# Low parts of the first two batches shared 3 to 5 between VectorE and GpSimd, and the first batch's keys and queries placed from SBUF to SBUF

## What is computed

```python
def reference(x, ctx1, ctx2, Wq, bq, Wk, bk, Wv, bv, Wp, bp, w_router, w_gating, w_gate, w_up, w_down):
    # x, ctx1, ctx2: (16, 256, 256)
    q = layernorm(x) @ Wq + bq
    k = concat([ctx1 @ Wk + bk, ctx2])            # 512 keys a batch
    v = concat([ctx1 @ Wv + bv, ctx2])
    attn = softmax(q k^T * 16 ** -0.5)            # per batch and head: 256 x 512
    x = x + (attn @ v) @ Wp + bp
    h = layernorm(x)
    cw = softmax(h @ w_router) * softmax(h @ w_gating / 0.1)
    cw = cw / (sum(cw) + 1e-9)                    # 8 weights a token
    for e in range(8):                            # w_gate, w_up: 256 x 1024, w_down: 1024 x 256
        x += cw[:, e] * ((silu(h @ w_gate[e]) * (h @ w_up[e])) @ w_down[e])
    return x
```

## Time and profile before

| | us |
|---|---|
| median of 3 runs | 2712.37 |
| lowest and highest | 2711.29, 2715.34 |
| the profiled execution, its own time | 2711.55 |
| its span in the trace | 2709.8 |
| mean granted TensorE clock | 0.991 of full |

### The profile page before, as it was taken

One profiled execution on the slowest core, in us unless ns is written; L12 is line 12 of the kernel. 1 busy time (PEld: TensorE's weight loads), 2 busy tenths in 40 slices (PEclk: granted clock), 3 DMA queues, 4 the chain that ended last, 5 costly groups with the idle time before them and its releaser, 6 DMA issues.

```text
span 2709.8 us, 46807 instructions
## 1 busy us (share of the span) xinstructions
PE 2660.4 (98%) x15969; PEld 2184.3 (81%) x15969; DVE 2007.7 (74%) x3303; ACT 1526.0 (56%) x2887; POOL 1651.8 (61%) x1837
## 2 busy tenths in 40 slices
PE   6899999999999999999999999999999999999998
PEld 5578888888888888888888888888888888888887
DVE  6987777777778777777777777777787777655554
ACT  4655555555555555555555555555555555544443
POOL 4766666666656666566666566666566666655554
PEclk8899999999999999999999999999999999999999
DMA  6344434444333443433434433444333442333332
GB/s 166 101 112 122 127 100 118 132 120 123 115 118 115 120 126 115 127 109 112 131 115 131 120 116 108 125 122 131 113 105 114 126 122 88 97 107 113 108 102 82
DMA packets 298427, 315.44 MB, mean 116 GB/s; under 512 B 22096, under 2 KB 269264, under 8 KB 298192
## 3 DMA queue, kind: packets, MB, share of 16 engines
q1 hardware_dynamic: 298192, 312.45, 39.0%
HBM read 278.15 MB, written 33.69 MB: 115 GB/s over the span
## 4 chain that ended last, share of the span: by engine, by line
PE 94%; DVE 4%; issue 1%; DMA 1%; POOL 0%; ACT 0%; SPq 0%; POOLq 0%; DVEq 0%; ACTq 0%
PE ps_s L706 26%; PE ps_t L706 26%; PE ps_o L740 25%; PE ps_s L803 4%; PE ps_t L813 4%; PE ps_a L782 2%; PE ps_a L784 2%; PE ps_m L586 1%; PE ps_m L615 1%; DVE negmax L1187 1%; PE ps_m L604 1%; DVE Pt_lo L1059 1%; PE ps_m L659 0%; DMA d_k<-kT_lo 0%; PE ps_m L677 0%
## 5 line engine op out<-in xcount | busy, mean ns | idle before, releaser
L969 DVE SCALAR_TENSOR_TENSOR hf<-hf,ps_s 128x512 f32<-128x512 f32 x512 | 350.2, 684 | 326.7 <-ACT hf L827 324.8
L833 ACT ACTIVATE h_hi<-ps_t 128x512 fp32r<-128x512 f32 x512 | 306.1, 598 | 440.2 <-DVE ps_t L976 440.2
L1221 POOL TENSOR_TENSOR wg_lo<-stage_w,wg_hi 128x512 fp32r<-128x512 f32 x256 | 330.9, 1292 | 339.5 <-ACT wg_hi L840 337.9
L827 ACT ACTIVATE hf<-ps_s 128x512 f32<-128x512 f32 x512 | 306.4, 598 | 410.5 <-PE ps_s L706 410.5
L981 DVE TENSOR_TENSOR h_lo<-ps_t,h_hi 128x512 fp32r<-128x512 f32 x512 | 353.0, 689 | 211.9 <-ACT h_hi L833 205.6
L740 PE MATMUL ps_o<-h_lo,wd_hi 128*128 128x512 f32 x1024 | 400.1, 391 | 0.0
L740 PE MATMUL ps_o<-h_hi,wd_hi 128*128 128x512 f32 x1024 | 398.5, 389 | 0.9 <-DVE h_lo L981 0.9
L740 PE MATMUL ps_o<-h_hi,wd_lo 128*128 128x512 f32 x1024 | 398.4, 389 | 0.0
L976 DVE TENSOR_TENSOR ps_t<-hf,ps_t 128x512 f32<-128x512 f32 x512 | 356.4, 696 | 52.9 <-PE ps_t L706 6.2
L1221 POOL TENSOR_TENSOR wd_lo<-stage_w,wd_hi 128x512 fp32r<-128x512 f32 x256 | 330.8, 1292 | 93.0 <-ACT wd_hi L840 93.0
L947 ACT ACTIVATE Pt<-ps_t 128x512 f32<-128x512 f32 x512 | 305.8, 598 | 142.1 <-PE ps_t L813 134.1
(11 more groups left out here) (208 smaller groups left out, 4734.3 us busy)
## 6 DMA issues: line engine op xcount, KB each, us to landing
stage_w<-in_L_ffn_w_gate_dram SPq DMA_DIRECT2D x256, 256.0 KB, 2.8
stage_w<-in_L_ffn_w_up_dram SPq DMA_DIRECT2D x256, 256.0 KB, 3.1
stage_w<-in_L_ffn_w_down_dram SPq DMA_DIRECT2D x256, 256.0 KB, 2.8
KTs<-d_k SPq DMA_DIRECT2D x96, 256.0 KB, 4.9
cwb<-d_cw SPq DMA_DIRECT2D x64, 256.0 KB, 3.6
QTs<-d_q SPq DMA_DIRECT2D x192, 64.0 KB, 2.7
X<-in_x_dram SPq DMA_DIRECT2D x32, 256.0 KB, 4.5
d_k<-kT_hi SPq DMA_DIRECT2D x16, 512.0 KB, 4.1
```

Source lines behind the costliest of these rows:

```text
L827: act.activation(hf[:], ps_g[:], ACT.Tanh, scale=0.5).then_inc(tanh_done, 1)
L833: act.activation(h_hi[f % FC][:], ps_u[:], ACT.Copy).then_inc(hh_done, 1)
L969: dve.scalar_tensor_tensor(out=hf[:], in0=hf[:], scalar=1.0, in1=ps_g[:], op0=ALU.add, op1=ALU.mult).then_inc(gate_done, 1)
L1221: pool.tensor_tensor(lo[:], raw_weights(n), hi[:].bitcast(F32), ALU.subtract).then_inc(wl_done, 1)
```

## The change

**The low parts.** For items of batches 0 and 1 DVE now takes items 1, 4, 6 of each eight, POOL 0, 2, 3, 5, 7. That is 4 low parts fewer on DVE and 4 more on POOL in each of the two batches, 8 in all. From batch 2 on the shares stay. The semaphores behind the low parts are counted with a running sum.

**The first batch's placing.** For batch 0 the way through DRAM is gone: `place_first` issues, pair by pair, 3 DMAs of keys (32 rows of 2 KB each) and 6 of queries (16 rows of 1 KB each) directly from `kT` and `qT` to `KTs` and `QTs`. These are 72 DMAs on SP, where the old way had 4 stores and 18 loads. PE waits for each pair's own semaphore (`first_in`). ACT and DVE may overwrite `kT` and `qT` for batch 1 only when all 72 have landed (`wait_stored`).

**Around it.** The 3 loads of the experts' weights move from `first_loads` to steps 20 to 22 of turn 0. Of the constant rows only 3 are loaded, and the transposed scores use 99 rows of `KTs` and `QTs` where they used 128. GpSimd's clearing of `key_rows` (0.53 us in the trace) is gone. The q of batch 0 goes to a bank of its own, `ps_t[1]`, and waits for no other projection.

```diff
--- before.py
+++ after.py
     DVE_LOW = (1, 3, 5, 7)
+    DVE_LOW_ALONE = (1, 4, 6)
...
+        first_in = [sem(f"first_in{p}") for p in range(PAIRS)]
...
+        def wait_stored(eng, turn, count):
+
+            if turn.b == 0:
+                for arrived in first_in:
+                    eng.wait_ge(arrived, 16 * 9)
+            else:
+                turn.wait(eng, count, -1, 32)
...
+                if (b, name) == (-1, "q"):
+                    items[b, step] = (name, k, d, None, [])
+                    continue
...
-            return ps_m[:] if one else ps_o[:, 1, :]
+            return ps_t[1][:] if one is None else ps_m[:] if one else ps_o[:, 1, :]
...
-        def by_dve(i):
-            return i % OCT in DVE_LOW
...
+        def by_dve(b, i):
+            alone = (b + 1) * STEPS <= START
+            return i % OCT in (DVE_LOW_ALONE if alone else DVE_LOW)
...
-                for n in range(3):
-                    load_weights(n, 0)
-                eng.wait_ge(const_ready, CONSTS)
-                eng.dma_start(KTs[TOP:P].bitcast(F32), key_rows[TOP:P].unsqueeze(1).broadcast_to([ROWS, PAIRS, NK])).then_inc(rows_in, 16)
+                eng.wait_ge(rows_set, 1)
+                eng.dma_start(KTs[TOP:USED].bitcast(F32), key_rows[TOP:USED].unsqueeze(1).broadcast_to([3, PAIRS, NK])).then_inc(rows_in, 16)
...
+            def place_first():
+
+                eng.wait_ge(k_l.sem, 2)
+                eng.wait_ge(m_l.sem, 1)
+                for pair in range(PAIRS):
+                    m, at = pair // GP, pair % GP * ROWS
+                    for slot, part in enumerate((kT_hi, kT_lo, kT_hi)):
+                        eng.dma_start(KTs[slot * ROWS:(slot + 1) * ROWS, pair, :].bitcast(F32),
+                                      part[at:at + ROWS, m, :].bitcast(F32)).then_inc(first_in[pair], 16)
+                    if pair == 0:
+                        eng.wait_ge(q_l.sem, 2)
+                        eng.wait_ge(const_ready, CONSTS)
+                    for slot, part in enumerate((qT_hi, qT_hi, qT_lo)):
+                        for h in range(2):
+                            to, row = slot * ROWS + h * HD, at + h * HD
+                            eng.dma_start(QTs[to:to + HD, pair, h, :].bitcast(F32),
+                                          part[row:row + HD, m, :].bitcast(F32)).then_inc(first_in[pair], 16)
...
+                    if turn.b == -1 and step == 10:
+                        place_first()
+                    if turn.b == 0 and step >= 20 and step - 20 < 3:
+                        load_weights(step - 20, 0)
...
+                        if turn.b + d == 0:
+                            if i % 4 == 0:
+                                pe.wait_ge(first_in[i // 4], 16 * 9)
...
-                        pe.matmul(key_bank(j)[:], KTs[:, pair, kc * P:(kc + 1) * P],
-                                  QTs[:, pair].rearrange("p h n -> p (h n)"),
+                        pe.matmul(key_bank(j)[:], KTs[0:USED, pair, kc * P:(kc + 1) * P],
+                                  QTs[0:USED, pair].rearrange("p h n -> p (h n)"),
...
-                        turn.wait(act, used, 0, 32)
+                        wait_stored(act, turn, used)
...
-                        turn.wait(dve, used, 0, 32)
+                        wait_stored(dve, turn, used)
```

More of the change, by code:

```diff
@@ L389, in tokens @@
             return xh[g % 2][:, :, k, :], xl[g % 2][:, :, k, :]
-        def by_dve(i):
-            return i % OCT in DVE_LOW
-        def low_parts(i, dve):
-            return sum(by_dve(j) == dve for j in range(i))
+        def by_dve(b, i):
+            alone = (b + 1) * STEPS <= START
+            return i % OCT in (DVE_LOW_ALONE if alone else DVE_LOW)
+        low_parts = {True: [0], False: [0]}
+        for b in range(B):
+            for i in range(STEPS):
+                for dve in (True, False):
+                    low_parts[dve].append(low_parts[dve][-1] + (by_dve(b, i) == dve))
         def raw_weights(n):
@@ L455, in place_queries @@
             def place_queries(turn, d, g):
[L457 removed]
+                turn.wait(eng, q_out, d - 1, 32)
                 turn.wait(eng, t_ps, d - 1, 2 * OCT * (g + 1))
[L459 to L460 removed]
                 pairs = slice(g * GP, (g + 1) * GP)
@@ L500, in body @@
                         combine_ahead(f)
[L501 to L509, removed]
-                    if turn.has(0) and step == 1:
-                        place_keys(turn, 0, 1)
-                    if turn.has(0) and step == 3:
-                        place_queries(turn, 0, 1)
+                    if turn.b == -1 and step == 10:
+                        place_first()
+                    if turn.b == 0 and step >= 20 and step - 20 < 3:
+                        load_weights(step - 20, 0)
+                    if turn.b >= 0 and turn.has(1):
+                        if step == 14:
+                            store_keys(turn, 1)
+                        if step == 15:
+                            store_queries(turn, 1)
+                        if step == 17:
+                            place_keys(turn, 1, 0)
+                        if step == 19:
+                            place_queries(turn, 1, 0)
+                    if turn.b >= 1 and turn.has(0):
+                        if step == 1:
+                            place_keys(turn, 0, 1)
+                        if step == 3:
+                            place_queries(turn, 0, 1)
                     if step in (10, 12) and turn.closed is not None:
@@ L808, in body @@
                         pair, kc = i // KC, i % KC
+                        if turn.b == 0 and i == 0:
+                            pe.wait_ge(rows_in, 16)
                         if kc == 0:
@@ L928, in body @@
                         turn.wait(act, m_ps, 1, 1)
-                        turn.wait(act, k_out, 0, 32)
+                        wait_stored(act, turn, k_out)
                         act.activation(kT_hi[:, :, N:NK], ps[:].rearrange("p (c n) -> p c n", n=N), ACT.Copy).then_inc(m_h.sem, 1)
@@ L1055, in low_part @@
                 d, i = item_at(step, -1)
-                if turn.has(d) and by_dve(i):
+                if turn.has(d) and by_dve(turn.b + d, i):
                     turn.wait(dve, exp_done, d, i + 1)
@@ L1147, in body @@
                         turn.wait(dve, m_h, 1, 1)
-                        turn.wait(dve, k_out, 0, 32)
+                        wait_stored(dve, turn, k_out)
                         dve.tensor_tensor(kT_lo[:, :, N:NK], ps[:].rearrange("p (c n) -> p c n", n=N),
@@ L1282, in body @@
                     d, i = item_at(step, -1)
-                    if turn.has(d) and not by_dve(i):
+                    if turn.has(d) and not by_dve(turn.b + d, i):
                         turn.wait(pool, exp_done, d, i + 1)
```

31 lines of the change are left out of this document (14 added, 17 removed).

## The result

| | us |
|---|---|
| before, median of 4 runs | 2711.83 (2710.78 to 2715.34) |
| after, median of 4 runs | 2741.22 (2740.57 to 2742.03) |
| ratio after / before | 1.0108, 95% interval 1.0093 to 1.0123 |
| span of the profiled execution | 2740.2, where it was 2709.8 |

The change makes the kernel 29 us slower. The forecast was 2718, the range ended at 2724. Each ratio further down is taken against runs of the kernel before that were made beside the experiment (medians 2712.58 to 2713.16).

The account below looks back on a forecast made before the run. The feed-forward, bound by PE, only shifts; ahead of it DVE sets the pace. Wait 3.0, clock 1.7, loop 1.2 and batch 1 and the rest 0 sum to +5.9 us, forecast 2718 us, range 2707 to 2724.

Parts of the forecast that it names:

- What bounds the kernel: Whole span: PE-bound feed-forward from 180 us is untouched and only shifts; ahead of it DVE sets the pace.
- The wait it adds: Start: ACT's read of batch 1's key projection waits for all 72 DMAs, 48.7 for 45.70 us; +3.0 us.
- 72 x 0.46 is 33.1 us: SP's issuing of the copies at 0.46 us each: the last issued at 46.5 us, landing at 48.7.
- the rival on the issue: SP issues copies within SBUF faster, at 0.37 us; the kernel takes 2706 us; chance 0.13.
- These cost nothing: Loads on SP behind the 72 copies, and the experts' weights: no cost, at most one landing (4.3 us).
- The clock behind the wait: PE, steps 5 to 12: idling during the wait brings a slow clock stretch; +1.7 us, ends 0 and 6.2.
- The low parts, DVE's side: From 60 us on: eight fewer low parts on DVE save 5.6 us at most.
- The loop behind them: Second half of batch 0: PE's values wait for POOL's split and low part; +1.2 us, ends -2 and +2.
- two maxima end 1.28 us later: Closing step of the loop through POOL on DVE: 3.90 + 1.28 = 5.2 us for four steps.
- Batch 1, taken at 0: Batch 1's eight groups, 6.4 us each, longer than the loop: 0 us, ends -2.8 and +1.
- The rest, taken at 0: 99 rows for 128 in the transposed scores, one POOL clearing less, 32 constant rows less to load: 0 us.
- the third: Rival, slower by more: +5 for the wait, +5 for the clock, +2 for the loop, 2724 us; chance 0.15.

Follow-up runs that it names:

- e7: Changed kernel with batch 0's keys and queries in own buffers, so ACT and DVE wait for none of the 72 copies; 2735.96 us, ratio 1.0084.
- e10: e7 with the old shares and the load of the second half of batch 1's VF issued by ACT; 2718.29 us, ratio 1.0018.
- e1: Changed kernel with the old shares of low parts (DVE items 1, 3, 5, 7 in every batch); 2732.91 us, ratio 1.0064.
- e6: Changed kernel with 185 useless transposes on PE at step 6 of batch 0, inside the wait for the copies; 2743.07 us, ratio 1.0109.
- e3: Changed kernel with the old shares and batch 0 placed through DRAM again, the other edits kept; 2711.38 us, ratio 0.9992.
- e8: Kernel before with 24 unread small DMAs on SP, in groups of four of one form, to price an issue; one execution, 2726.27 us.
- e11: e3 with only the first pair placed directly from SBUF to SBUF, between the stores and the loads back; 2708.76 us, ratio 0.9989.
- e4: Changed kernel with the old shares, first four pairs placed directly (36 DMAs for 72), four through DRAM; 2718.23 us, ratio 1.0017.
- e5: Kernel before with low parts 3, 5, 7 of each eight on DVE in batches 0 and 1; 2712.47 us, ratio 0.9996.
- e2: Kernel before with only the new shares (1, 4, 6 on DVE in batches 0 and 1); 2721.19 us, ratio 1.0025.
- e12: e2 with six idle matmuls on PE in every second step of four in batches 0 and 1; 2721.86 us, ratio 1.0035.

## Why the prediction was wrong, point by point

- **What bounds the kernel: right.** The feed-forward begins later and takes as long as before (+30.91 at item 104, +31.05 at item 511).
- **The wait it adds: right in place and mechanism, wrong in size, and this is most of the miss.** ACT's read of batch 1's keys and all that stands behind it waited as described. The term that failed is "72 x 0.46 is 33.1 us". The 0.46 came from DMAs that read DRAM, and the copies have SBUF on both sides: 0.63 measured, 45.6 us for 72. With 1.5 us in which SP itself stalled (the third DMA of the first pair took 1.73) ACT came to read at 61.72 and not at 48.7: +16.1 us at item 12 instead of +3.0. The first score, at 21.47 where 19.7 was forecast, was late for the same two reasons. The landing, in contrast, was shorter than the 2.2 us taken: 1.8 to 2.0. The ends that were set for this term, 0.9 and 5.1, varied the issue only downwards and the landing upwards; and the rival on the issue knew only quicker copies.
- **"These cost nothing" for the loads behind the 72: wrong, though hidden.** After the change the wait on ACT covers them. Lift that wait and they show: 15.29 us for `VF` in e7, 10.3 for the queries of batch 1 in e10.
- **The clock behind the wait: smaller than +1.7 where it was put, and more later.** From item 12 to 23 e1 lost 0.9 us. e6 lost 2.2 there where the kernel after lost 3.6, but it began 0.8 us later, so that almost nothing was left of it. But e1 lost 2.5 more between items 39 and 47, where PE had the next projections at a granted clock of 0.50. Here is e1 there, and e3 at the same work:

```profile
100.00:104.00 4.00, 4.00 (x42) 3.18 (x43) 3.22 (x6) 2.25 (x4) 2.93 (x7) 0.50 0.78 184
```

```profile
80.00:84.00 4.00, 3.77 (x49) 3.02 (x50) 3.85 (x7) 2.66 (x7) 3.28 (x7) 1.00 0.88 204
```

  At 0.50 PE is busy for 4.00 of 4 us and DVE waits; at 1.00 both keep up, and e3 lost 0.2 us there. Other kernels fit this: with items 3 and 7 on DVE the stretch from item 39 to 47 took 10.6 and 10.8 us at a mean clock of 1.00 (before, e3), 11.5 to 12.3 at 0.85 and 0.86 (e8, e11, e10), and 13.1 to 13.2 at 0.74 to 0.77 (e1, e4, e5). That the clock is the cause is read from these rows, and no run isolates it; nor is it settled what holds the clock down so long after the wait. In the kernel after it needs no clock: with the new shares the stretch took 13.4 us at 0.88 (after, e6), at 0.92 and 0.93 (e7, e2) and at 1.00 (e12), so there the loop alone accounts for the loss.
- **The low parts, DVE's side: wrong as an upper bound that could count.** Relief of DVE was worth nothing (e5), though DVE's timeline had no gap. From item 23 to 35 e5's groups took 15.3 us for 15.5 together; then it lost 2.5 us from item 39 to 47, and the next group gave 2.0 back. One possible reason is that the chain through POOL and PE paces the groups nearly as much as DVE's load, another the lower clock (0.77 for 1.00 from item 39 to 47). Neither is shown. DVE's work itself did shrink as costed. From 60 to 166 us its low parts have a median of 686 ns before and 693 in e2, and a mean of 833 ns before, 877 in e2 and 899 in e5: 8 of 35 took over 1 us before and 9 of 26 in e2. So DVE kept the long ones and gave away short ones, but over the two batches 24 at 877 or 899 ns for 32 at 833 are still 5.6 or 5.1 us less (an estimate), where 5.6 was the price. That some are long agrees with the rule named from the Trainium skill (SBUF — State Buffer, "Who interferes with whom"). It shows on POOL's side in e12 as well: the last of the four small splits takes 0.68 us beside DVE's low part (71.17 to 71.85), where the others take 0.20 to 0.26. That fits the 0.2 us by which the split took longer than costed.
- **The loop behind them: right mechanism, size wrong by a factor of three to five.** Forecast +1.2 in the second half of batch 0 with -2 and +2 as ends. Items 23 to 39 cost e2 6.0 us, and 3.6 at full clock (e12); 1.4 had been lost before item 23. The step that failed here is "two maxima end 1.28 us later": DVE's other work falls between these two maxima once the loop sets the pace. With it, 5.2 us a group become 5.4 in the two without statistics or normalisation on DVE, and 6.8 and 6.9 in the two with. At half the clock the stretches on PE in the loop are longer besides, which the prediction did not foresee for this place.
- **Batch 1, taken at 0: wrong in its first steps.** e2 and e12 lose 2.4 and 2.5 us from item 39 to 104, and all of it by item 47 (the projections again). Behind that, where DVE's sums and statistics fill the groups, 0 was right.
- **The rest, taken at 0: a gain of 3.4 us in the table, 1.8 in the medians (e3)**, that after the change is waited away. With the bank for q and the later weights the loads back begin 4.3 us earlier than before, 3.3 earlier than in e2, which has the old start. Which of the two edits does it was not tried.

The sum against what was measured, in us: wait 3.0 and 16.1; clock 1.7 and 4.5 (e1 from item 12 to 104, the clock's share of it not isolated); low parts 1.2 and 9.8. Together 5.9 and 30.4, of 30.9 in the trace and 29.4 in the medians. None of the rivals was it: the third had the sign, but made its 2724 from the clock and the landing, not from the issue.

## What to carry to other kernels

Before many small DMAs replace a few large ones, multiply their count by the price of an issue of exactly that form, and where no row of the trace has the form (here SBUF on both sides), leave that price open upwards as well as downwards, since it is multiplied by the count. Then list everything that stands on the same queue behind them: lifting the wait that shows uncovers the next. And to relieve a busy engine, move work that nothing waits for, though even that gained nothing here (e5); an engine that receives a piece on the way from maximum to values makes a loop, and what the relieved engine still does then falls into that loop's gaps.

## What was not expected of the hardware

A DMA from SBUF to SBUF takes SP 0.59 us to issue, 0.63 from start to start, against 0.42 and 0.46 with DRAM on one side, whether 16, 32 or 128 partitions are touched (e8; with DRAM, 32 and 128). The granted clock fell to 0.50 long after the start, in a part where PE was busy for 17 of 20 us (140 to 160 us after the change, 16.97 busy at 0.50). Behind item 39 a fallen clock cost a kernel with the new shares nothing that can be told: e2 (0.91 in the mean up to item 104) and e12 (0.98) lose 2.4 and 2.5 us there. Between items 23 and 39, by the same comparison, it cost e2 about 2.4 us.
